# Running-maximum matmuls on one half of the array's rows beside the score matmuls on the other half, with the units laid in a new order

## The reference

```python
qh = proj(q, W_q, b_q); kh = proj(k, W_k, b_k); vh = proj(v, W_v, b_v)   # 16 heads of 8
scores = einsum('bhqd,bhkd->bhqk', qh, kh) / sqrt(8)
scores = where(m == 0, -1e9, scores)
attn = softmax(scores, axis=-1)
context = einsum('bhqk,bhkd->bhqd', attn, vh)
```

## Time and profile before

| | us |
|---|---|
| median of three timed executions | 821.77 |
| the profiled execution's own time | 817.71 |
| its span | 815.8 |
| PE (TensorE) busy | 700.3 |
| DVE (VectorE) busy | 564.3 |
| ACT (ScalarE) busy | 515.7 |
| POOL (GpSimd) busy | 260.3 |

### The profile page before, as it was taken

One profiled execution on the slowest core, in us unless ns is written; L12 is line 12 of the kernel. 1 busy time (PEld: TensorE's weight loads), 2 busy tenths in 40 slices (PEclk: granted clock), 3 DMA queues, 4 the chain that ended last, 5 costly groups with the idle time before them and its releaser, 6 DMA issues.

```text
span 815.8 us, 19683 instructions
## 1 busy us (share of the span) xinstructions
PE 700.3 (86%) x7289; PEld 484.9 (59%) x7289; DVE 564.3 (69%) x1227; ACT 515.7 (63%) x787; POOL 260.3 (32%) x304
## 2 busy tenths in 40 slices
PE   3699999975568898899899999998999998699997
PEld 3577777763215566556655655665665565467776
DVE  5799999977766887877877878777767674511111
ACT  4577777763254776776776786777777767344431
POOL 3488888881251203213221230231232020000000
PEclk9899999997557999999999999999999999599999
DMA  3122222434526167247336535733754470111110
GB/s 132 38 76 92 98 75 75 141 96 45 114 56 143 29 142 160 55 108 159 85 78 155 114 84 120 159 73 89 161 104 100 83 175 2 45 38 32 53 39 23
DMA packets 59504, 74.39 MB, mean 91 GB/s; under 512 B 35336, under 2 KB 40194, under 8 KB 59450
## 3 DMA queue, kind: packets, MB, share of 16 engines
q1 hardware_dynamic: 59450, 73.65, 37.9%
HBM read 32.61 MB, written 1.40 MB: 42 GB/s over the span
## 4 chain that ended last, share of the span: by engine, by line
PE 56%; DVE 27%; issue 9%; ACT 5%; POOL 2%; DVEq 1%; ACTq 0%
DVE mx L1511 10%; PE ps L718 8%; PE ps L632 6%; PE ps L778 6%; PE ps L790 6%; PE ps L618 6%; PE ps L705 6%; PE ps L624 4%; PE ps L518 3%; DVE ss L1217 3%; DVE rden L1520 2%; PE ps L532 2%; PE ps L655 2%; ACT arena L855 2%; DVE arena L1237 2%
## 5 line engine op out<-in xcount | busy, mean ns | idle before, releaser
L1511 DVE TENSOR_REDUCE mx<-ps 128x1 f32<-128x500 f32 x336 | 216.8, 674 | 77.5 <-PE ps L632 75.2
L967 ACT ACTIVATE P<-ps,kbias,kscale 125x896 f32<-125x896 f32 x192 | 210.1, 1097 | 48.2 <-PE ps L705 44.2
L632 PE MATMUL ps<-KP,Qb 128*128 128x500 bf16 x336 | 131.9, 393 | 17.5 <-DVE mx L1511 14.3
L718 PE MATMUL ps<-P,Vp 125*32 125x112 f32 x3072 | 113.4, 265 | 2.0 <-ACT P L967 1.3
L1062 POOL TENSOR_TENSOR KP<-kvall,KP 128x1500 bf16<-128x1500 f32 x16 | 48.6, 3036 | 196.3 <-ACT KP L911 196.3
L518 PE MATMUL ps<-wkv,cT 128*125 128x256 f32 x384 | 92.0, 383 | 0.7 <-ACT arena L868 0.7
L718 PEld LDWEIGHTS ps<-P,Vp 125*32 125x32 f32 x3072 | 67.1, 109 | 40.3 <-issue 29.3
L518 PEld LDWEIGHTS ps<-wkv,cT 128*125 128x125 f32 x384 | 69.5, 190 | 9.8 <-issue 1.0
L705 PEld LDWEIGHTS ps<-QS,KS 128*128 128x128 bf16 x768 | 55.5, 99 | 32.2 <-issue 16.6
L705 PEld LDWEIGHTS ps<-QS,arena 128*128 128x128 bf16 x768 | 53.3, 98 | 32.7 <-issue 20.2
L705 PE MATMUL ps<-QS,KS 128*128 128x112 bf16 x768 | 69.8, 214 | 3.5 <-DVE QS L1517 2.5
(11 more groups left out here) (204 smaller groups left out, 1058.3 us busy)
## 6 DMA issues: line engine op xcount, KB each, us to landing
cT<-ctxT_dram SPq DMA_DIRECT2D x32, 750.0 KB, 4.4
KS<-KP SPq DMA_DIRECT2D x48, 375.0 KB, 7.2
arena<-KP SPq DMA_DIRECT2D x48, 375.0 KB, 7.3
QS<-QD SPq DMA_DIRECT2D x96, 28.0 KB, 5.7
wgu<-w_dram SPq DMA_DIRECT2D x8, 256.0 KB, 3.1
silu<-w_dram SPq DMA_DIRECT2D x8, 256.0 KB, 2.9
x<-xh_dram SPq DMA_DIRECT2D x1, 512.0 KB, 3.5
mixed<-att SPq DMA_DIRECT2D x16, 28.0 KB
```

What stands on the lines that cost most here:

```text
L632: ins = nc.tensor.matmul(ps[:, bank, 0:KCW], q[:, 128 * c:128 * c + 128], KP[par][0][:, KCW * k:KCW * k + KCW], start=True, stop=True)
L718: ins = nc.tensor.matmul(ps[r:r + PW, 7, c:c + PAIRW], Vp[par][0:TK, t, p, :], P[t % 2][0:TK, PAIRW * p:PAIRW * p + PAIRW], start=(t == 0 ...
L967: nc.scalar.activation(P[t % 2][0:TK, :].rearrange("p (k n) -> p k n", k=2), src, ACT.Exp, scale=kscale[0:TK, bass.ds(n, 1)], bias=kbias[0 ...
L1511: ins = v.tensor_reduce(mx[:, c, k:k + 1], ps[:, bank, 0:KCW], AX.X, ALU.max)
```

## The change

The heads are put in another order: all even heads first, then all odd ones (`halves`, in the mask from which `Qb` is formed). The rows of keys and queries already have all even heads' dimensions in rows 0 to 63 and the odd ones' in rows 64 to 127. Now

- the scores of a half tile are eight matmuls on 64 rows by 56 columns (one for each head of one parity, all into one bank) instead of four on 128 rows by 112 columns. `QS` is half as wide, `QD` has one copy instead of two masked ones, and `pmask` and its load are gone;
- 18 of the 21 maxima are matmuls on 64 rows (`BLOCKS`), alternately on rows 0 to 63 and 64 to 127; the last three, whose block holds heads of both parities, stay on 128 rows;
- `SH` leaves its two pieces in rows 0 and 64 and they are copied to rows 0 and 64 of `QS`; this copy waits also for the DMAs that stack `QS`;
- `weigh` reads its 112 moving columns as two runs of 56;
- `PLACES` is laid anew: one maximum after the first half of the scores and one after `weigh`, all other units between the second half and `weigh`; the VectorE steps of the feed-forward hang on other maxima.

```diff
 MXS = [f"MX{n}" for n in range(CH * KC)]
+BLOCKS = ([(c + 4 * h, k, HALF * h, HALF) for c in range(CH // 2) for k in range(KC) for h in range(2)]
+          + [(CH // 2, k, 0, 128) for k in range(KC)])
 PLACES = [
-    [["MX0", "MX1", "V0"], ["MX2", "MX3", "AT"], ["DEN", "MX4", "V1"], ["MX5", "DE", "V2"],
-     ["MX6", "WO", "K0"], ["MX7", "MX8", "MX9"], ["MX10", "MX11", "K1"], ["MX12", "MX13", "MX14"],
-     ["MX15", "XT", "K2"], ["MX16", "MX17", "MX18"], ["MX19", "MX20", "G"], ["SH", None, None]],
-    [["MX0", "MX1", "V0"], ["MX2", "U", "MX3"], ["DEN", "MX4", "V1"], ["MX5", "MX6", "V2"],
-     ["MX7", "WO", "K0"], ["MX8", "MX9", "HT"], ["MX10", "MX11", "K1"], ["MX12", "DN", "MX13"],
-     ["MX14", "MX15", "K2"], ["MX16", "MX17", "MX18"], ["MX19", "MX20", "LT"], ["SH", None, "Q1"]],
+    [[["MX0"], ["V0"], ["MX1"]], [["MX2"], ["AT"], ["MX3"]], [["MX4"], ["DEN"], ["MX5"]],
+     [["MX6"], ["V1"], ["MX7"]], [["MX8"], ["DE"], ["MX9"]], [["MX10"], ["K0"], ["MX11"]],
+     [["MX12"], ["K1"], ["MX13"]], [["MX14"], ["V2"], ["MX15"]], [["MX16"], ["K2"], ["MX17"]],
+     [["MX18"], ["XT", "WO"], ["MX19"]], [["MX20"], ["G"], []], [["SH"], [], []]],
+    [[["MX0"], ["V0"], ["MX1"]], [["MX2"], ["U"], ["MX3"]], [["MX4"], ["DEN"], ["MX5"]],
+     [["MX6"], ["V1"], ["MX7"]], [["MX8"], ["K0"], ["MX9"]], [["MX10"], ["HT"], ["MX11"]],
+     [["MX12"], ["K1"], ["MX13"]], [["MX14"], ["DN"], ["MX15"]], [["MX16"], ["K2"], ["MX17"]],
+     [["MX18"], ["V2", "WO"], ["MX19"]], [["MX20"], ["LT"], []], [["SH"], [], ["Q1"]]],
 ]
...
-        QD = [[sb(f"QD{n}_{k}", [128, 2, S], BF16) for k in range(3)] for n in range(2)]
+        QD = [[sb(f"QD{n}_{k}", [128, S], BF16) for k in range(3)] for n in range(2)]
-        QS = [sb(f"QS{n}", [128, HQ], BF16)[:] for n in range(2)]
+        QS = [sb(f"QS{n}", [128, HQ2], BF16)[:] for n in range(2)]
...
-                    c, k = divmod(int(unit[2:]), KC)
+                    c, k, r, n = BLOCKS[int(unit[2:])]
-                    ins = nc.tensor.matmul(ps[:, bank, 0:KCW], q[:, 128 * c:128 * c + 128],
-                                           KP[par][0][:, KCW * k:KCW * k + KCW], start=True, stop=True)
+                    ins = nc.tensor.matmul(ps[:, bank, 0:KCW], q[r:r + n, 128 * c:128 * c + 128],
+                                           KP[par][0][r:r + n, KCW * k:KCW * k + KCW], start=True, stop=True)
...
-                for p in range(4 * k, 4 * k + 4):
+                rows = slice(HALF * k, HALF * k + HALF)
+                for p in range(NPAIR):
                     c0 = S2 * p + TK * t
-                    ins = nc.tensor.matmul(ps[:, 2 * (t % 2) + k, PAIRW * (p % 4):PAIRW * (p % 4) + PAIRW],
-                                           KS[par][:, c0:c0 + 128], QS[par][:, PAIRW * p:PAIRW * p + PAIRW],
-                                           start=True, stop=True)
+                    ins = nc.tensor.matmul(ps[:, 2 * (t % 2) + k, S * p:S * p + S], KS[par][rows, c0:c0 + 128],
+                                           QS[par][rows, S * p:S * p + S], start=True, stop=True)
...
+                heads = P[t % 2][0:TK, :].rearrange("p (k q s) -> p q k s", k=2, q=NPAIR)
-                                           P[t % 2][0:TK, PAIRW * p:PAIRW * p + PAIRW],
+                    ins = nc.tensor.matmul(ps[r:r + PW, 7, c:c + PAIRW], Vp[par][0:TK, t, p, :], heads[:, p, :, :],
...
+                    dve.wait_ge(sem(f"stacked{par}"), loads(b, par, 2 * STACK))
                     for k in range(2):
-                        r = ONES + 32 * k
-                        ins = v.tensor_copy(QS[par][ONES:ONES + 1, HQ2 * k:HQ2 * k + HQ2],
-                                            ps[r:r + 1, bank, 0:HQ2])
+                        r = HALF * k
+                        ins = v.tensor_copy(QS[par][r:r + 1, :], ps[r:r + 1, bank, 0:HQ2])
...
-                        elif unit == "MX6":
+                        elif unit == "MX10":
                             first_sum(n)
-                        elif unit == "MX8":
+                        elif unit == "MX12":
                             quantise(n)
-                        elif unit == "MX10":
+                        elif unit == "MX14":
                             quantised(n)
...
-                        elif unit == "MX4":
+                        elif unit == "MX5":
                             hidden_steps(at, n)
-                        elif unit == "MX6":
+                        elif unit == "MX7":
                             hidden_quantised(n)
-                        elif unit == "MX16":
+                        elif unit == "MX17":
                             normed(n)
...
-        "hmask1_in": np.repeat(np.eye(H, dtype=f), DK, axis=0)[order],
+        "hmask1_in": np.repeat(np.eye(H, dtype=f), DK, axis=0)[order][:, halves],
```

More of the change, by code:

```diff
@@ L46 @@
 STRIDE = 8
-ONES = 0
 TWO_ONES = 1.0 + 127 * 2.0 ** -16
@@ L56 @@
 MXS = [f"MX{n}" for n in range(CH * KC)]
+BLOCKS = ([(c + 4 * h, k, HALF * h, HALF) for c in range(CH // 2) for k in range(KC) for h in range(2)]
+          + [(CH // 2, k, 0, 128) for k in range(KC)])
 PLACES = [
[6 rows of a table removed]
[8 rows of a table added]
 ]
-ALL = [[u for places in half for u in places if u] for half in PLACES]
+ALL = [[u for places in half for place in places for u in place] for half in PLACES]
 ENDS = ["DEN", "WO"]
@@ L186, in build @@
 def build(nc, xh, ctxT, m0, m1, gates, rows, bq, bk, wkv0, wq0, dense0, wg0, wu0, wd0, wq1, wk1, wv1, wo1,
-          gatew, w1, b1, w2, b2, bv, ident_in, hmask_in, hmask1_in, pmask_in,
+          gatew, w1, b1, w2, b2, bv, ident_in, hmask_in, hmask1_in,
           den_sel_in, rank_in, out):
@@ L217, in build @@
         hmask1 = sb("hmask1", [128, H])
-        pmask = sb("pmask", [128, 2])
         bv_sb = sb("bv_sb", [128, 2])
@@ L377, in _ @@
             for dst, src in ((dense_sb[:], dense0), (wgu[:, 0, :], wg0), (wgu[:, 1, :], wu0), (wdn[:], wd0),
-                             (mi[0:TK, :], m1), (hmask1[:], hmask1_in), (pmask[:], pmask_in),
+                             (mi[0:TK, :], m1), (hmask1[:], hmask1_in),
                              (bv_sb[:], bv), (bq_sb[:], bq), (bk_sb[:], bk), (wq1_sb[:], wq1), (wk1_sb[:], wk1),
@@ L433, in stack @@
                     sp.dma_start(spread(QS[par], j).rearrange("r (p n) -> r p n", p=NPAIR),
-                                 QD[par][part][:].rearrange("p k s -> p (k s)")).then_inc(sem(f"stacked{par}"), 16)
+                                 QD[par][part][:]).then_inc(sem(f"stacked{par}"), 16)
             def pair1(i):
@@ L474, in _ @@
             sp.wait_ge(sem("out_done"), 16)
-        LATE = 18 * 16
+        LATE = 17 * 16
         @block.tensor
@@ L626, in fill @@
                 elif unit[:2] == "MX":
-                    c, k = divmod(int(unit[2:]), KC)
-                    if c == 0 and k == 0:
+                    c, k, r, n = BLOCKS[int(unit[2:])]
+                    if unit == MXS[0]:
                         pe.wait_ge(sem("qb_ready"), b + 1)
@@ L715, in weigh @@
                     pe.wait_ge(sem("o_ready"), b)
+                heads = P[t % 2][0:TK, :].rearrange("p (k q s) -> p q k s", k=2, q=NPAIR)
                 for p in range(NPAIR):
                     r, c = PW * (p % 4), PAIRW * (p // 4)
-                    ins = nc.tensor.matmul(ps[r:r + PW, 7, c:c + PAIRW], Vp[par][0:TK, t, p, :],
-                                           P[t % 2][0:TK, PAIRW * p:PAIRW * p + PAIRW],
+                    ins = nc.tensor.matmul(ps[r:r + PW, 7, c:c + PAIRW], Vp[par][0:TK, t, p, :], heads[:, p, :, :],
                                            start=(t == 0 and p < 4), stop=(t == T - 1), skip_group_check=True)
@@ L725, in window, with units_at @@
                 w = 2 * i + par
[L727 to L732, removed]
+                def units_at(t, place):
+                    for unit in PLACES[par][t][place]:
+                        if unit in units(at):
+                            b = (w - 1 if unit in ENDS else w + 2 if unit[0] == "K" else i + 2 if unit in CHAIN
+                                 else w + 1)
+                            fill(at, unit, b, par if unit[0] == "K" else 1 - par)
                 first = first_pair and par == 0
@@ L736, in window @@
                     scores(at, t, 0, first)
-                    unit_at(t, 0)
+                    units_at(t, 0)
                     scores(at, t, 1, first)
-                    unit_at(t, 1)
+                    units_at(t, 1)
                     if t > 0:
@@ L743, in window @@
                         weigh(w - 1, 1 - par, T - 1, first_pair)
-                    unit_at(t, 2)
+                    units_at(t, 2)
             pe.wait_ge(sem("filled"), 1)
@@ L984, in pair1 @@
                             take_sums(w - 1)
-                        for unit in PLACES[par][t]:
+                        for unit in [u for place in PLACES[par][t] for u in place]:
                             if unit not in has:
@@ L1083, in queries @@
```

(13 more changed lines are left out.)

## The result

The changed kernel takes 834.04 us (median of 4, 825.03 to 834.33) against 821.03 for the kernel before (median of 4): ratio 1.0147, interval 1.0108 to 1.0186. It is slower by 12 us by the ratio, 13 by the medians; I had forecast 20 us faster. One of the four runs took 825.03 us, at a mean granted clock of 0.933 where the other three had 0.917 to 0.924. All of the loss lies in the sixteen windows.

The account below looks back on a forecast made before the run. TensorE bounds the kernel, VectorE close behind. Even windows -13.8 us, odd -0.6, windows 12 to 14 -5.7, window 15 +0.3: total -19.8 on 817.71, giving 798; the timed median lies 4 above, 802, stated as 801, range 791 to 812.

Parts of the forecast that it names:

- Maxima beside scores: TensorE's window tiles: a maximum next to scores of the other rows costs nothing, -3.8 us a window.
- Scores cut in two: Half tile of scores: eight matmuls of 56 columns take 0.21 us against 0.20, +0.2 us a window.
- Switches: Changes between 64-row and 128-row work on TensorE cost 0.1 us each, +1.6 us a window.
- The new order and VectorE: TensorE's waiting for VectorE: 4.4 us even (4.7 before), 5.0 odd (3.1 before); windows become 27.3 and 28.3 us.
- What costs nothing: `SH`'s added wait, half-width `QD`, `weigh` in two runs, earlier V and K, and the prologue's maxima: no cost.
- rival D: Windows: 64-row matmuls give no overlap, 836 us, or half tiles keep 50 ns loads, 834 us; chance 0.23.

Follow-up runs that it names:

- experiment 7: Changed kernel with TensorE's windows as straight code and all 21 maxima on 128 rows, so none runs beside scores: 865.8 us, ratio 1.056 to the kernel before.
- experiment 5: Changed kernel with TensorE's windows as straight code and V0 of even windows moved behind `weigh`: 809.11 us, ratio 0.9873 to the kernel before.
- 6: Kernel before with the new order of units alone, on 128 rows and 112 columns as before: 818.95 us, ratio 0.9987.
- experiment 8: Kernel of experiment 5 with V1 moved beside `DEN` in both windows and V2 of odd windows into tile 3: 798.8 us, ratio 0.9755 to the kernel before.
- experiment 1: Changed kernel with TensorE's eight window pairs written out as straight code, other engines keeping their loop: 811.26 us, ratio 0.9907 to the kernel before.
- 11: Changed kernel, looped, with six of the eight products of `weigh` left out in tiles 1 to 10 (output incomplete), 1459 records: 818.68 us.
- 1619: Changed kernel, looped, with four of the eight products of `weigh` left out in tiles 1 to 10 (output incomplete): 838.93 us.
- 1779: Changed kernel, looped, with two of the eight products of `weigh` left out in tiles 1 to 10 (output incomplete): 828.32 us.

## Why the prediction was wrong

**Maxima beside scores: right.** Nothing was paid for a maximum next to the other rows' scores; removing the overlap and adding the borders that come with it costs 54 us (7).

**Scores cut in two: right.** In the tile shown above the sixteen scores start 26 ns apart, as taken.

**Switches: right.** Taken 0.1 us; the changed kernel shows 0.08 at the unit behind the second half, and experiment 7 0.1.

**The new order and VectorE: right for odd windows, off for even ones.** Odd windows 28.7 for 28.3. Even windows without a stop and with V0 repaired 28.4 for 27.3. Below I add up TensorE's idle gaps in the trace; the ends of matmuls are modelled there, so the gaps are shorter than the waits of my reckoning, and only their changes are compared. An odd window has 2.3 us before and 4.3 in experiment 5, 2.0 more where I had reckoned 1.9 more; an even window has 2.9 and 3.8, 0.9 more where I had reckoned 0.3 less. The rest of the window, TensorE's stream, fell by 1.7 and 2.0 to 2.1, for 2.0 forecast. On the old matmuls the order added nothing (6: gaps of 2.3 and 2.9 us as before): VectorE's waits came only with the shorter stream. That the tiles behind `DEN` and `U` could be mended is shown by 8, which moved two units; in even windows V1 beside `DEN` alone brought 0.4 us.

**"What costs nothing": this step failed.** Two entries were missing from it.

- 192 more matmuls and as many loads in each turn of TensorE's loop (1557 to 1939 records). The loop of the kernel before fetched no code between 362 and 542 us; the new one fetches in every turn and stops 3.2 to 3.6 us at each of three jumps back, and the work behind each runs at the lower clock. Windows 4, 6 and 8 lose 15.8 us together against experiment 1. From start to start the three stops take 10.3 us where experiment 1 takes 1.9, so 8.4 of the 15.8 are the stops and an estimated 7.4 are what follows them, the half clock above all. The changed kernel loses 23 in all (834.04 to 811.26); most of the rest is window 13 (4.3 us) and window 10 (1.0), where half clock stands without a jump back. I counted what the added instructions cost in streaming and never what they cost as code.
- V0. I wrote that V and K come earlier in the tile and that only ScalarE reads them. Their bank 6 is also Q1's, and VectorE empties Q1 only behind `MX0`. Ahead of `weigh`, V0 stops TensorE for 1.0 to 1.1 us in each even window and delays P for the next tile: the first two exponentials of window 6 start 3.32 us apart in experiment 1 and 2.67 in experiment 5.

From first to last `SH` the windows take 424.4 us before and 441.6 after. Without the stops they take 420.1 (1), with V0 repaired 416.4 (5), with V1 and V2 moved 405.1 (8). Forecast was 404; experiment 8 comes near it by an order of units that the prediction did not have, which is no proof of its sum. The sign and the time (834) were those of rival D, by coincidence: its mechanism, no overlap, did not occur; the last line of the prediction named a new wait for bank 6 as what would make it wrong, and that wait is there. The stop at the jump was in none of the cases.

Not settled: no run takes the lower clock away and leaves the stops, so the 7.4 us are an estimate; and it is open why half clock also appears where no stop of 3 us stands before it, in window 13 of the changed kernel, in window 10 of experiment 5 and in window 4 of experiments 7 and 11.

## What to carry to other kernels

Count instructions as code, not only as time: before a change splits matmuls inside a loop, compare the body with what still runs without instruction fetches, and look for the fetch queue on the page. When a unit is moved, follow its bank to its last reader on every engine, not only to its own. Row groups are worth having for small contractions, if work on all rows is kept out from between them; put work that does not need VectorE beside VectorE's longest operation, when VectorE is nearly as full as TensorE.

## What the runs showed that I had not expected

The limit is narrow: 1557 records cost nothing, 1619 cost two stops at each jump back (3.4 and 2.9 us), and the smaller body, 1619, is slower than the larger, 1779 (838.93 against 828.32). A stop with 2.9 us of idle time on TensorE is followed by a granted clock of 0.50 to 439.00, past the first tile, so a wait for code is paid a second time in the work behind it.
